# A hybrid block on one core: the attention's softmax divided with queries on partitions, and the norms' small arithmetic on VectorE

## The reference, cut to what matters

```
a  = layernorm(x);  xn = layernorm(a) * ln_g + ln_b         # two roots, one behind the other
# state-space branch: 128 channels x 64 states, a scan over 512 tokens
h  = exp(dt[:, :, None] * A) * h + (dt * xt)[:, :, None] * bt[:, None, :];  y = sum_n h * c
# attention branch: 16 heads of 8 features on 4 key heads, blocks of 32 queries that see 96 keys
attn = softmax(scores + bias);  ao = attn @ v3;  attn_out = ao @ wo
# convolution of 4 taps with silu; memory: softmax(a @ dec.T) @ dec
r  = a + 0.2 * attn_out + 0.45 * ssm_out + 0.15 * conv_out + 0.2 * mem_out
x  = x + r;  x = x + layernorm(x) @ int4(w) + bias + lora
```

## Time and profile before

| | |
|---|---|
| median of 3 runs | 1114.3 us (1114.25 to 1122.23) |
| the profiled execution | 1114.23 us |
| its span, first to last instruction | 1112.4 us |
| busy in the span: PE, DVE, ACT, POOL | 830.9, 979.3, 837.5, 955.6 us |
| mean granted clock of PE | 0.871 of 2.4 GHz |
| first scan starts at | 38.68 us |
| DMA | 181.18 MB, 16 engines busy 61% |

### The profile page before, as it was taken

One profiled execution on the slowest core, in us unless ns is written; L12 is line 12 of the kernel. 1 busy time (PEld: TensorE's weight loads), 2 busy tenths in 40 slices (PEclk: granted clock), 3 DMA queues, 4 the chain that ended last, 5 costly groups with the idle time before them and its releaser, 6 DMA issues. The chain is left out here.

```text
span 1112.4 us, 19145 instructions
## 1 busy us (share of the span) xinstructions
PE 830.9 (75%) x4151; PEld 339.3 (30%) x4151; DVE 979.3 (88%) x2299; ACT 837.5 (75%) x2255; POOL 955.6 (86%) x675
## 2 busy tenths in 40 slices
PE   5367878688777786877778777867868778677775
PEld 2023333233323332333323333323332333232332
DVE  2688999979997999979999699897999799999991
ACT  4468886788778878687877887679887887858871
POOL 6369988989898988988899898899989898979892
PEclk9556998978997989979898798888899798989897
DMA  5845667647675666666676476665666566766630
GB/s 111 196 126 169 180 159 185 171 138 198 163 183 155 185 167 159 172 157 172 168 203 161 128 191 162 167 173 159 177 176 183 153 187 165 188 161 164 196 95 9
DMA packets 124391, 181.18 MB, mean 163 GB/s; under 512 B 29263, under 2 KB 41056, under 8 KB 124256
## 3 DMA queue, kind: packets, MB, share of 16 engines
q1 hardware_dynamic: 123968, 179.56, 61.4%
q10 hardware_dynamic: 288, 0.20, 0.1%
HBM read 170.79 MB, written 5.05 MB: 158 GB/s over the span
## 5 line engine op out<-in xcount | busy, mean ns | idle before, releaser
L1389 POOL TENSOR_TENSOR prod<-hst,C 128x1024 f32<-128x1024 f32 x256 | 602.0, 2354 | 94.9 <-DVE hst L1201 94.4
L1201 DVE TENSOR_TENSOR_SCAN hst<-decay,bank 128x512 f32<-128x512 f32 x384 | 459.5, 1209 | 3.0 <-DVE cv_a L1236 2.8
L1189 DVE TENSOR_TENSOR bank<-bank,B 128x512 f32<-128x512 f32 x384 | 263.1, 685 | 52.6 <-PE bank L911 34.8
L665 ACT ACTIVATE decay<-wide,A_rep 128x512 f32<-128x512 f32 x384 | 273.4, 715 | 41.5 <-DVE hst L1201 31.2
L911 PE MATMUL bank<-spread,sel_bc 96*128 96x512 bf16 x384 | 164.5, 434 | 101.0 <-DVE hst L1201 90.6
L679 ACT ACTIVATE prob<-s_sb,nmax 128x96 f32<-128x96 f32 x512 | 185.2, 365 | 0.9 <-DVE nmax L1214 0.5
L1405 POOL TENSOR_TENSOR uwide<-uwide,B 128x512 f32<-128x512 f32 x128 | 162.7, 1271 | 22.5 <-DMA uwide<-u_rows 22.5
L935 PE MATMUL bank<-prod,sel_red 128*32 128x512 f32 x1024 | 164.9, 722 | 0.0
L1201 DVE TENSOR_TENSOR_SCAN hst<-bank,uwide 128x512 f32<-128x512 f32 x128 | 155.4, 1214 | 2.7 <-POOL uwide L1405 2.7
L951 PE MATMUL bank<-ident,prob 128*96 128x128 f32 x512 | 85.9, 295 | 77.5 <-ACT ao L695 58.3
L944 PE MATMUL bank<-k,q 128*128 128x384 f32 x256 | 126.7, 580 | 22.3 <-DVE nmax L1214 22.2
(11 more groups left out here) (189 smaller groups left out, 1027.4 us busy)
## 6 DMA issues: line engine op xcount, KB each, us to landing
wide<-dt_rows SPq DMA_DIRECT2D x512, 256.0 KB, 4.7
uwide<-u_rows SPq DMA_DIRECT2D x128, 256.0 KB, 4.1
spread<-parts SPq DMA_DIRECT2D x66, 32.0 KB, 4.1
x_sb<-in_L_attn_x_dram SPq DMA_DIRECT2D x8, 256.0 KB, 4.5
dt_rows<-sp_t SPq DMA_DIRECT2D x8, 256.0 KB, 2.6
out_dram<-outb SPq DMA_DIRECT2D x8, 256.0 KB, 3.9
vw<-v_tok SPq DMA_DIRECT2D x80, 16.0 KB, 3.3
u_rows<-uv SPq DMA_DIRECT2D x8, 64.0 KB, 2.4
```

Source lines behind the costliest of these rows:

```text
L665: nc.scalar.activation(to, wide[m % SLOTS][:, s % 2, :], ACT.Exp, scale=A_rep[:, g:g + 1]).then_inc(exp_done, 1)
L1189: v.tensor_tensor(uP[s % 4][:, :], uP[s % 4][:, :], B2[p][:, :], ALU.mult).then_inc(dbx_done, 1)
L1201: v.tensor_tensor_scan(hst[:, s % 8, :], kept, into[:, :], 0.0, ALU.mult, ALU.add).then_inc(scan_done, 1)
L1389: g.tensor_tensor(prod[:, 2 * (m % 4):2 * (m % 4) + 2, :], hst[:, 2 * (m % 4):2 * (m % 4) + 2, :], C2[p][:, :].unsqueeze(1).to_broadcast([ ...
```

## The change

The probabilities go into the transposes undivided. PE multiplies by the values; ACT copies the undivided result (`raw_copy`); PE transposes it to queries on partitions (`turn`, into columns 384 to 511 of sP); DVE multiplies by the inverse sums, 128x32 at a time (`output_norm`), into `ao_q`. When all 16 blocks are there PE transposes four times (`heads`), ACT copies with the factor 0.2 (`heads_copy`), and `project` n = 6 to 9 works on pieces of 128 columns against `wo4`, which holds wo four times. Lags: transposes at S+6, values and `raw_copy` at S+8, inverse at S+8, `turn` at S+10, `output_norm` at S+11. Since PE writes the bank that the scores lie in, `scores_there` also waits for `turned`, and `scores` for `ao_norm`. POOL's `prob_norm` is gone.

In the norms POOL keeps one power each: over 8 columns for both roots of the first norm, s = var / (var + eps) + eps giving the second, and over 4 for the other norm. Additions, the reciprocal, the product and the shifts are DVE instructions. `normalise2` stands at slot 21, `ln_apply` and `scale_xn` one slot later than before.

The sixteen loads of `wo4` stand at the end of SP's front, and DVE clears `wo4`.

```diff
-LAST_PROJECT = {60: (0, 1), 61: (2, 3), 62: (4, 5), 63: (6, 7)}
+LAST_PROJECT = {60: (0, 1), 61: (2, 3), 62: (4, 5)}
...
-    "normalise2": 20, "ffn": 25, "output": 29,
...
-    "ln_stats": 0, "ln_aggr": 2, "ln_root": 4, "ln_apply": 11, "scale_xn": 12, "softplus_exp": 20,
+    "shift2": 20, "normalise2": 21, "ffn": 25, "output": 29,
+
+    "ln_stats": 0, "ln_aggr": 2, "ln_vars": 3, "ln_root": 6, "ln_shift": 10, "ln_apply": 12, "scale_xn": 13, "softplus_exp": 20,
...
-VALUE_DMA_AT = {4: (0, 1, 2, 3, 4, 5), 5: (6, 7, 8), 6: (9, 10, 11)}
+VALUE_DMA_AT = {3: (0, 1, 2, 3, 4, 5), 4: (6, 7, 8), 5: (9, 10, 11)}
...
-BIAS_LAG, EXP_LAG, INV_LAG, NORM_LAG, PT_LAG, PT_COPY_LAG, PV_LAG, AO_COPY_LAG = 2, (3, 4), 6, 5, 9, 9, 11, 11
+BIAS_LAG, EXP_LAG, INV_LAG, PT_LAG, PT_COPY_LAG, PV_LAG, RAW_COPY_LAG, TURN_LAG, NORM_LAG = 2, (3, 4), 8, 6, 6, 8, 8, 10, 11
+TURN_AHEAD = 3
...
-    ["stats", "aggr", "ve", "nm", "r", "nb", "vr", "vrr", "ve2", "r2", "xa", "xn"])}
+    ["stats", "aggr", "t", "inv", "ratio", "s", "r", "nb", "xa", "xn"])}
...
                 assert n == N_W_DMA
+
+            def load_output_weights():
+
+                sp.wait_ge(wo_clean, 1)
+                for c in range(4):
+                    for g in range(KVH):
+                        sp.dma_start(wo4[32 * c + g * HD:32 * c + g * HD + HD, c, :, :],
+                                     wo[g * REP * HD:(g + 1) * REP * HD, :].rearrange("(r h) e -> h r e", r=REP)) \
+                            .then_inc(w_in, 16)
...
+                load_output_weights()
...
+                    wait(act, pt_ready, B * NBLK + k - 1)
+                    wait(act, p_inv, B * NBLK + k - 3)
...
-            def ao_copy(B, k):
+            def raw_copy(B, k):
                 wait(act, pv_ready, B * NBLK + k + 1)
-                if k == 0:
-                    wait(act, ready["t"], B * N_TAIL - N_TAIL + 1)
-                nc.scalar.activation(ao4[:, :, k * W:(k + 1) * W],
-                                     ptP[:, 0:128].rearrange("p (r q) -> p r q", r=REP), ACT.Copy).then_inc(ao_evac, 1)
+                wait(act, turned, B * NBLK + k - 1)
+                nc.scalar.activation(ao_raw[:, k % 2, :], ptP[:, 0:128], ACT.Copy).then_inc(raw_evac, 1)
+
+            def heads_copy(B):
+                wait(act, heads_ready, B + 2)
+                nc.scalar.activation(aoT[:, :, :, :].rearrange("p c r q -> p (c r q)"), ptP[:, :], ACT.Copy,
+                                     scale=RW_ATTN).then_inc(heads_evac, 1)
...
+                        if s == 0:
+                            heads_copy(B - 1)
...
+                wait(pe, ao_norm, B * NBLK + max(0, k - TURN_AHEAD))
...
-                wait(pe, p_norm, B * NBLK + k + 1)
-                wait(pe, ao_evac, B * NBLK + k)
+                wait(pe, p_exp, B * NBLK + k + 1)
+                wait(pe, raw_evac, B * NBLK + k)
+                if k == 0:
+                    wait(pe, heads_evac, B)
...
+            def turn(B, k):
+
+                wait(pe, raw_evac, B * NBLK + k + 1)
+                wait(pe, ao_norm, B * NBLK + k)
+                nc.tensor.transpose(sP[:, KVH * 3 * W:], ao_raw[:, k % 2, :], ident[:, :]).then_inc(turned, 1)
+
+            def heads(B):
+
+                wait(pe, ao_norm, (B + 1) * NBLK)
+                transposes([ao_q[:, 4 * a:4 * a + 4, :].rearrange("p k c -> p (k c)") for a in range(4)], 128, 128, ptP) \
+                    .then_inc(heads_ready, 1)
...
-                    wait(pe, ao_evac, (B + 1) * NBLK)
-                    ins = mm(jobP[:, :], wo_p[:, n - 6, :], ao4[:, n - 6, :], start=False, stop=False)
+                    wait(pe, heads_evac, B + 1)
+                    c = n - 6
+                    for r in range(REP):
+                        ins = mm(jobP[:, :].rearrange("p (a c q) -> p a c q", a=4, c=4)[:, :, c, :], wo4[:, c, r, :],
+                                 aoT[:, :, r, :], start=False, stop=False, skip_group_check=True)
...
+                    k = block_at(s, TURN_LAG)
+                    if k is not None:
+                        turn(B, k)
+                    if s == UNITS - 1:
+                        heads(B)
...
-                for n in range(8, N_PROJ - 1):
+                for n in range(6, N_PROJ - 1):
...
+            def ln_vars(B, n):
+
+                wait(dve, ln_step, B * N_LN + LN["aggr"] + n)
+                if n == 0:
+                    ins = v.tensor_scalar(vv[:, 0:NT], mv[:, :, 1], EPS, None, ALU.add)
+                if n == 1:
+                    ins = v.reciprocal(vi[:, :], vv[:, 0:NT])
+                if n == 2:
+                    ins = v.tensor_tensor(vi[:, :], mv[:, :, 1], vi[:, :], ALU.mult)
+                if n == 3:
+                    ins = v.tensor_scalar(vv[:, NT:2 * NT], vi[:, :], EPS, None, ALU.add)
+                ins.then_inc(ln_step, 1)
+
+            def ln_shift(B):
+
+                wait(dve, ln_step, B * N_LN + LN["r"])
+                v.scalar_tensor_tensor(nb[:, :], mv[:, :, 0], -1.0, rr[:, 0:NT], ALU.mult, ALU.mult).then_inc(ln_step, 1)
...
+                v.memset(wo4[:, :, :, :], 0.0).then_inc(wo_clean, 1)
...
+                for n in range(4):
+                    ln_vars(B, n)
+                ln_shift(B)
...
 
                 wait(dve, s_ready, B * NBLK + k + 1)
                 wait(dve, p_exp, B * NBLK + k - 1)
+                if k >= TURN_AHEAD:
+                    wait(dve, turned, B * NBLK + k - TURN_AHEAD + 1)
...
             def inverse_sums(B, k):
                 wait(dve, p_exp, B * NBLK + k + 1)
-                wait(dve, p_norm, B * NBLK + k - 3)
                 v.reciprocal(pinv[:, k % 4, :], psum_r[:, k % 4, :]).then_inc(p_inv, 1)
+
+            def output_norm(B, k):
+
+                wait(dve, turned, B * NBLK + k + 1)
+                wait(dve, p_inv, B * NBLK + k + 1)
+                wait(dve, heads_ready, B)
+                v.tensor_tensor(ao_q[:, k, :].rearrange("p (g h) -> p g h", h=HD),
+                                sP[:, KVH * 3 * W:].rearrange("p (g c) -> p g c", c=W)[:, :, 0:HD],
+                                pinv[:, k % 4, :].unsqueeze(2).to_broadcast([128, KVH, HD]), ALU.mult).then_inc(ao_norm, 1)
...
+            def vars2(B):
+
+                wait(dve, l2_step, B * N_L2 + L2["aggr"])
+                v.tensor_scalar(vz[:, :], mv2[:, :, 1], EPS, None, ALU.add).then_inc(l2_step, 1)
+
+            def shift2(B):
+
+                wait(dve, l2_step, B * N_L2 + L2["r"])
+                v.scalar_tensor_tensor(nbz[:, :], mv2[:, :, 0], -1.0, rz[:, :], ALU.mult, ALU.mult).then_inc(l2_step, 1)
...
                             aggr2(B - 1)
+                            vars2(B - 1)
+                        if s == AT["shift2"]:
+                            shift2(B - 1)
...
+                        if 0 <= s - AT["ln_vars"] < 4:
+                            ln_vars(B + 1, s - AT["ln_vars"])
+                        if s == AT["ln_shift"]:
+                            ln_shift(B + 1)
...
-            def ln_root_step(B, n):
-
-
-                o, a, b, op = ((ve, mv[:, :, 1], eps_t, ALU.add), (nm, mv[:, :, 0], mone, ALU.mult),
-                               (rr, ve[:, :], mhalf, ALU.pow), (nb, nm[:, :], rr, ALU.mult),
-                               (vr, mv[:, :, 1], rr, ALU.mult), (vr, vr[:, :], rr, ALU.mult),
-                               (vr, vr[:, :], eps_t, ALU.add), (rr2, vr[:, :], mhalf, ALU.pow))[n]
-                wait(pool, ln_step, B * N_LN + LN["aggr"] + n)
-                g.tensor_tensor(o[:, :], a, b[:, :], op).then_inc(ln_step, 1)
+            def ln_roots(B):
+
+                wait(pool, ln_step, B * N_LN + LN["s"])
+                g.tensor_tensor(rr[:, :], vv[:, :], mhalf[:, :], ALU.pow).then_inc(ln_step, 1)
...
-            def prob_norm(B, k):
-                wait(pool, p_inv, B * NBLK + k + 1)
-                g.tensor_tensor(prob[:, k % 4, :, :], prob[:, k % 4, :, :],
-                                pinv[:, k % 4, :].unsqueeze(2).to_broadcast([128, KVH, 3 * W]), ALU.mult) \
-                    .then_inc(p_norm, 1)
...
             def root2(B):
-                for n, (o, a, b, op) in enumerate(((vz, mv2[:, :, 1], eps_t, ALU.add), (nmz, mv2[:, :, 0], mone, ALU.mult),
-                                                   (rz, vz[:, :], mhalf, ALU.pow), (nbz, nmz[:, :], rz, ALU.mult))):
-                    wait(pool, l2_step, B * N_L2 + L2["aggr"] + n)
-                    g.tensor_tensor(o[:, :], a, b[:, :], op).then_inc(l2_step, 1)
+
+                wait(pool, l2_step, B * N_L2 + L2["t"])
+                g.tensor_tensor(rz[:, :], vz[:, :], mhalf[:, 0:NT], ALU.pow).then_inc(l2_step, 1)
```

82 lines of the change are left out of this document (36 added, 46 removed).

## The result

The changed kernel takes 1224.7 us (median of 4 runs, 1217.43 to 1228.8) against 1114.8 (4 runs): 1.096 times as long, interval 1.089 to 1.103. The forecast was 1158 in a range of 1108 to 1180: the sign was right, and 67 us, well over half of the loss, were not in it. The granted clock of PE fell from 0.871 to 0.827.

The account below looks back on a forecast made before the run. DVE was taken to bound the kernel, by its own work and its waits. Six middle batches at +4.8 (+28.8), batch 0 +3.6, batch 7 +7.0, start +3.0, tail +1.5: +43.9 on 1114.3, so 1158, range 1108 to 1180.

Parts of the forecast that it names:

- The stall at slot 24: DVE's waits for PE and ACT around slot 24 vanish through the earlier normalise2: -6.0 us per middle batch.
- output_norm, +1.4: Sixteen 32-element DVE instructions per batch, at 0.09 us each: +1.4 us (1.0 to 2.9).
- The 1166 by the Trainium skill: Alternative total if each output_norm costs 0.16 us, by the skill's price for a PSUM source.
- The holds, +6.5 and 0.5 for the instructions: Norms' small DVE instructions: 0.5 us themselves, 6.5 us waiting for POOL's running instruction to end, per middle batch.
- The rival "not held" (1121): Small DVE instructions slip past POOL without waiting, so the 5.2 us per middle batch go: 1121 us, chance 0.20.
- The 1.3 I took off for waits that they cover: Existing DVE waits for PE in slots 4 to 7, hidden under the holds: 6.5 becomes 5.2 per batch.
- The wait for `turned`, +3.5: DVE's bias_and_max waits for PE's new transpose, at blocks 4, 8, 11 and 12: +3.5 us per middle batch.
- The start and batch 0, +6.6 together: Start waits for wo's sixteen loads, less a shorter first-norm chain, +3.0; batch 0, without second norm, +3.6 us.
- Batch 7, +7.0: Last batch, without first norm and with only 0.6 us of slot 24 waits to lose: +7.0 us.
- Tail, +1.5: End of the program: heads transposes, their copy and latencies, +1.5 us.
- The rival "PE or ACT takes over in slots 20 to 29": ACT's exponential of unit 24 late again, PE's transposes delay slot 29: +3 a batch, 1179 us, chance 0.12.

Follow-up runs that it names:

- tasv1: Changed kernel with `turn` one PE slot earlier, norms' arithmetic back on POOL, wo's loads on their own semaphore, values' loads early: 1123.6 us, ratio 1.009.
- tsv1: Changed kernel with `turn` one PE slot earlier, wo's loads on their own semaphore, values' loads early: 1168.0 us, ratio 1.046.
- th1: Changed kernel with `turn` one PE slot earlier and the norms' five held DVE instructions in single columns: 1157.2 us, ratio 1.038.
- h3: tsv1 with the norms in single columns, POOL's second-norm power, its shift and normalise2 earlier, ACT's logarithm five slots later: 1087.4 us, ratio 0.973.
- the probe: Kernel before the change plus twelve forms of small scratch DVE instruction (1 or 4 elements) where POOL's product is under way: 1146.5 us, one run.
- l1: tsv1 with ACT's logarithm, its two table loads and what follows from it five slots later: 1127.5 us, ratio 1.009.

## Why the prediction was wrong in size

- **The stall at slot 24, -6.0: right in what it named.** The reciprocal waits no more. I left the stretch behind it as it was (slot 29 at its 1.5); it waits 1.5 (slot 26), 2.4 (29) and 2.2 us (32) a batch now.
- **output_norm, +1.4: right.** 0.163 long, but the next instruction starts 0.08 after it (378.55, 378.63), 1.3 a batch. The 1166 by the Trainium skill ("VectorE: DVE Perf Modes", the TRN2 errata) took the length for the pace: that length is in the row, the pace isn't.
- **The holds, +6.5 and 0.5 for the instructions: right.** vz, nbz, vv, vi, nb and the two free ones take 6.8 us in a middle batch (2.15 + 1.68 + 1.26 + 0.75 + 0.69 + 0.29), against 7.0. (These are batch 2's; the mean is 6.7.) The rival "not held" (1121) falls. What was forecast as 1 to 2 us for all five is so for vz and nbz alone; vv, vi and nb have 0.6 to 0.9. The 1.3 I took off for waits that they cover was a misreading: before, the waits for L911 outside slot 24 lie mostly in slots 0 to 2 and 8, and only 0.3 us a batch in slots 4 to 7. Slots 0 to 7 together wait 1.9 us now, 1.3 before.
- **The wait for `turned`, +3.5: the step that failed.** DVE's waits for `turn`, by timeline and slot, are 11.5 us in a middle batch, less 2.0 that the same slots waited for scores before: 9.5. I read the slack of every block from PE's lead before ("others find 0.2 to 2 us of slack; 0.1") and wrote down for blocks 4, 8 and 12 0.65 each. Block 11 was right (1.45; 1.30 measured). Of the three, block 8 (slot 32) waits 2.2, block 4 (slot 20) 1.9, put down to ACT for the most part, and block 12 nothing; and the blocks that I gave slack, 3, 6, 7 and 15 (slots 17, 26, 29, 53), wait 7.0 together, 1.5 of it also before. The lead is not kept: `turn` follows a copy on ACT that stands behind the table loads, and that copy follows values that wait for their loads. Moving `turn` alone (t1) is worth 78 us. Of the 9.2 us a middle batch that the forecast lacked (13.96 for 4.8), this wait is 6, the waits of slots 0 to 7 are 1.8, ACT's at slot 20 1.6 and at slot 25 0.5, while slot 8's 0.6 went.
- **The loads of the values, not priced at all: PE stands 4.0 us at slot 14.** The step moved by three slots and its DMAs by one step of SP, behind a load that waits for a scan; I did not look at that queue. Moving them gave 10 us by itself (v1, not clear of the spread), and 24 behind t1 with POOL's norms (tasv1).
- **The start and batch 0, +6.6 together: 13.6.** DVE waits 3.3 for wo in slot 6, 1.9 for PE and 5.6 for ACT's setup (2.6 before) in slot 8; the rest is `turned`, as in the other batches. Batch 7, +7.0: 12.6, by the same wait. Tail, +1.5: 0.3.
- **The rival "PE or ACT takes over in slots 20 to 29", 1179 at 0.12,** was the nearest in mechanism, and priced too low: +21 over the forecast, where moving the logarithm and what follows from it gives back 35. It saw the low clock, but gave no price for it.

The sign came out because DVE's added work did (8.4 forecast, 8.2 measured in a middle batch); of the waits only those of slot 24 and of block 11 did. What stays open: why a kernel with fewer waits can be slower (t1 to tsv1, t1 to th1). The traces show the place, slot 29 with 0 or 3.7 us, and that it goes with PE's clock in the feed-forward matmuls; what puts the stretches of low clock before or over these matmuls was not tried by itself.

## What to carry to other kernels

A new wait must be priced by what its producer waits for after the change, followed back through every engine and the DMA queue, not by the lead that the producer's engine had before. When engines run in lock-step, price a stretch as one: the same edit was worth 10 or 24 us by what else was late there, and another pair of such edits cost 21. Look for the one long item that several waits lead back to (here a logarithm with two table loads) and move that first. Before a wait is explained by its queue, compare the granted clock of that place between batches of one run. On DVE beside a busy POOL, write small arithmetic on single columns, or with an operand in PSUM.

## What was unexpected of the hardware

- One column escapes the hold: `tensor_scalar` on 128x1 took 0.121 us beside POOL's product, on 128x4 0.586; in h3 the forms with a scalar operand in SBUF took 0.20 as 128x1, where the probe's 128x4 took 0.73.
- What a stretch of low clock costs a later engine: in tsv1, behind a stand of 2.84 us, the fp32 matmuls of the feed-forward layer took 2.07 and 1.22 us at a granted clock of 0.50, in place of 1.12 and 0.71 at 1.00, and DVE was idle for 3.80 us at the end. In l1's batch 4 the same came without a stand of PE over 1.3 us in the slots before.
